# A planner's charge for TensorE's turns between kinds of matmul, in an attention and expert feed-forward kernel

## The reference, cut to what matters

```python
def _L0_xattn_ref(query, key, value, mask, Wq, Wk, Wv, Wo, Wg, bg):   # 2048 queries, 1601 keys, 16 heads of 16
    q, k, v = (heads of query @ Wq.T, key @ Wk.T, value @ Wv.T)
    scores = jnp.einsum('bhqd,bhkd->bhqk', q, k) / jnp.sqrt(jnp.float32(dk))
    scores = jnp.where(mask[:, None, None, :] == 0, neg_inf, scores)
    scores = jnp.where(future[None, None, :, :], neg_inf, scores)
    attn = jnp.nan_to_num(jax.nn.softmax(scores, axis=-1), nan=0.0)
    context = jnp.einsum('bhqk,bhkd->bhqd', attn, v)
    gate = jax.nn.sigmoid(query @ Wg.T + bg)
    return gate * context @ Wo.T
def _L0_ffn_ref(x, gate_w, w1, w2, w3):                                # 8 experts of 128, two per token
    scores = jax.nn.softmax(xf @ gate_w, axis=-1)
    scale = (the two largest scores of a token, 0 elsewhere)
    xs = scale.T[:, :, None] * xf[None, :, :]
    h = jax.nn.silu(einsum('etd,edh->eth', xs, w1)) * einsum('etd,edh->eth', xs, w3)
    return einsum('eth,ehd->etd', h, w2).sum(axis=0)
x = x + _L0_xattn_ref(_layernorm(x), ctx_1024, ctx_1024, mask_BxS2_ik0, ...)
x = x + _L0_ffn_ref(_layernorm(x), ...)
```

## Time and profile before

| | us |
| --- | --- |
| median of 3 runs | 680.01 |
| lowest and highest of them | 677.1, 682.3 |
| span of the profiled execution, first to last instruction | 676.9 |
| TensorE matmul busy | 644.6 (95%) |
| VectorE busy | 471.3 (70%) |
| ScalarE busy | 379.5 (56%) |
| POOL busy | 230.4 (34%) |

### The profile page before, as it was taken

The page is one execution under the profiler, slowest core; times in us unless marked ns, Lnnn a source line. Parts: engine busy times, 40 slices in busy tenths (PEclk is TensorE's granted clock), DMA queues, the critical chain, the costliest instruction groups (busy, mean ns, idle before and its releaser), DMA issues.

```text
span 676.9 us, 13559 instructions
## 1 busy us (share of the span) xinstructions
PE 644.6 (95%) x5320; PEld 393.0 (58%) x5320; DVE 471.3 (70%) x981; ACT 379.5 (56%) x778; POOL 230.4 (34%) x283
## 2 busy tenths in 40 slices
PE   7887999999999999999999999999999999979997
PEld 3363565555565545554565556455456766768885
DVE  6637779998989999999989987412205533676454
ACT  2221456766646676667646677877784565123332
POOL 5005212522123115021005033385434434536662
PEclk9878799999999999999999899999999999999999
DMA  6985982010260000010093010102101021104100
GB/s 170 234 133 115 138 144 31 2 22 24 69 68 1 3 1 3 1 65 2 14 161 109 2 34 3 35 2 78 32 32 32 17 63 49 31 16 109 48 32 31
DMA packets 29305, 36.58 MB, mean 54 GB/s; under 512 B 5833, under 2 KB 16457, under 8 KB 29242
## 3 DMA queue, kind: packets, MB, share of 16 engines
q1 hardware_dynamic: 26248, 34.53, 24.6%
q10 hardware_dynamic: 946, 0.92, 0.4%
q0 software_dynamic: 2048, 0.27, 0.3%
HBM read 25.58 MB, written 8.06 MB: 50 GB/s over the span
## 4 chain that ended last, share of the span: by engine, by line
PE 45%; DVE 12%; ACT 3%; POOL 2%; issue 1%; DVEq 0%; ACTq 0%; POOLq 0%
PE bank L1600 9%; DVE pmax L1303 9%; PE bank L1578 8%; PE bank L1664 4%; PE bank L1666 4%; PE bank L1665 4%; PE bank L1429 3%; PE bank L1545 3%; PE bank L1685 2%; PE bank L1686 2%; ACT probs L1160 2%; PE bank L1688 2%; DVE xn_sb L1274 1%; PE bank L1610 1%; PE bank L1583 1%
## 5 line engine op out<-in xcount | busy, mean ns | idle before, releaser
L1160 ACT ACTIVATE probs<-bank 128x512 f32<-128x512 f32 (+4 forms) x592 | 283.2, 555 | 147.0 <-PE bank L1578 87.5
L1303 DVE TENSOR_REDUCE pmax<-bank 128x1 f32<-128x512 f32 (+6 forms) x640 | 322.7, 574 | 29.4 <-PE bank L1549 15.9
L1578 PE MATMUL bank<-qaug,kaug 64*128 64x512 f32 (+4 forms) x592 | 151.6, 455 | 2.5 <-DVE pmax L1303 1.1
L1600 PE MATMUL bank<-probs,vaug 128*32 128x256 f32 (+4 forms) x2048 | 142.3, 390 | 2.2 <-ACT probs L1160 1.8
L1545 PE MATMUL bank<-kaug,qaug 62*128 62x512 f32 (+6 forms) x640 | 135.0, 404 | 9.8 <-DVE stage L807 3.4
L1578 PEld LDWEIGHTS bank<-qaug,kaug 64*128 64x128 f32 (+1 forms) x592 | 66.2, 183 | 85.7 <-ACT probs L1160 29.8
L1545 PEld LDWEIGHTS bank<-kaug,qaug 62*128 62x128 f32 x640 | 76.5, 189 | 40.7 <-DVE pmax L1303 21.0
L1600 PEld LDWEIGHTS bank<-probs,vaug 128*32 128x32 f32 (+1 forms) x2048 | 52.3, 109 | 53.3 <-ACT probs L1160 18.4
L1032 POOL TENSOR_TENSOR h_lo<-v_sb,h_hi 128x512 fp32r<-128x512 f32 x31 | 40.1, 1295 | 66.3 <-ACT h_hi L1216 66.3
L1396 DVE SCALAR_TENSOR_TENSOR v_sb<-t_sb,v_sb 128x512 f32<-128x512 f32 x32 | 24.2, 757 | 45.2 <-POOL v_sb L1028 38.2
L1216 ACT ACTIVATE h_hi<-v_sb 128x512 fp32r<-128x512 f32 x32 | 20.4, 637 | 57.4 <-DVE v_sb L1396 55.5
(11 more groups left out here) (143 smaller groups left out, 824.4 us busy)
## 6 DMA issues: line engine op xcount, KB each, us to landing
qaug<-s_dram SPq DMA_DIRECT2D x32, 256.0 KB, 3.4
qaug<-q_parts SPq DMA_DIRECT2D x18, 256.0 KB, 9.2
q_parts<-stage SPq DMA_DIRECT2D x7, 512.0 KB, 2.9
k_parts<-stage SPq DMA_DIRECT2D x4, 512.0 KB, 5.0
w_sb<-in_w SPq DMA_DIRECT2D x4, 512.0 KB, 10.0
out<-x_sb SPq DMA_DIRECT2D x8, 256.0 KB, 2.3
ctx_sb<-in_ctx_t SPq DMA_DIRECT2D x3, 512.0 KB, 6.4
x_sb<-in_x SPq DMA_DIRECT2D x3, 512.0 KB, 6.3
```

Of the source, the lines that this page charges most:

```text
L1160: act.activation(probs[0:rows, u % NSLOT, h, off:CH], bank_of(e)[0:rows, off:CH], ACT.Exp, scale=DK ** -0.5).then_inc(act_read, 1)
L1303: dve.tensor_reduce(pmax[:, n % 2, qt, h, slot:slot + 1], bank[:, 0:w], AX_X, ALU.max).then_inc(dve_read, 1)
L1578: last.append(pe.matmul(pair[side][0][0:r, off:CH], keys_at(b, ROWS, hp, P * j, r), qaug[b:b + ROWS, p % 2, hp, off:CH], start=True, stop= ...
L1600: last = pe.matmul(psum[O_BANK][32 * h:32 * h + 32, q0:q1], vaug[0:r, col:col + 32], probs[0:r, u % NSLOT, h, q0:q1], start=(j == 0), stop ...
```

## The change

Two constants of the planner. `SWITCH`, the delay of a step's start at a turn, goes from 100 ns to 0. `TURN`, the time that a turn adds to the step's end, goes from 150 to 140 ns into values and from 270 to 200 ns into scores; into other kinds it stays at 200.

```diff
-RELOAD, SWITCH, HOP, LOAD, PIECE = 107, 100, 2500, 9000, 3000
+RELOAD, SWITCH, HOP, LOAD, PIECE = 107, 0, 2500, 9000, 3000
 SPREAD = 0.6
-TURN = {"values": 150, "scores": 270, "other": 200}
+TURN = {"values": 140, "scores": 200, "other": 200}
```

## The result

The changed kernel takes 673.34 us in the median of 11 runs (669.82 to 682.9), the kernel before 680.33 in 11 runs (677.1 to 682.97). The ratio is 0.9913, 95% interval 0.989 to 0.9937: faster, by 0.9%, where 3% had been forecast. The profiled execution has a span of 670.2 us, for 676.9.

A forecast was written before the change was run, and what follows sets the result against it. No engine alone was taken to bound the middle: TensorE, VectorE and ScalarE wait for each other's turn at banks. Early 81, middle 390, late 183 and 3.6 us sum to 657.6 us of span, so a 660 us median, range 640 to 684.

The forecast's parts named there:

- The middle: From the second head group's last maximum to the last of all: 339.5 us TensorE work plus 50 waiting, 390 us.
- 47 of the 72 us: Middle's waiting before: 274 overcharged turns at about 0.17 us; near nothing after, the remaining 25 us doubled to 50.
- The early stretch: Up to the second head group's last maximum: set by loads and first projections, 81 us, at most 3 us either way.
- I take 9 us: 183 us: After the last maximum: 173.7 us of TensorE work plus 9 us waiting, where before 24 us were waited on 218.5.
- The 7 us on 86: Late stretch before, after the last scores, with experts and last chunk's routing: about 7 us waiting on 86.
- 42 us of passes beside 50 us: First eight experts: POOL's 42 us is under the 50 us of TensorE work between the first and last of them.
- The sum: Whole span: 81 + 390 + 183 + 3.6 = 657.6 us, for 676.9 before; the median about 660.
- A: Rival: VectorE alone sets the middle's pace, which stays 350 us; 621 us in all; chance 0.08.
- C: Rival, slower: waiting stays 21% of the middle, by rhythm of seven banks and in-order queues; 430 us, 701 total; chance 0.10.
- B: Rival: turns only replace waits, 20 us more work and 20 less waiting; 680 us (673 to 687); chance 0.12.

The follow-up runs named there:

- e17: The change with the last chunk's reads on ScalarE and the planner charged the score, values and turn prices the trace shows: 681.7 us, 1.001 against the kernel before.
- p_145_200: The change with 145 instead of 140 ns for a turn into values: 676.3 us, 0.994 against the kernel before.
- e1: The kernel before with only the start delay `SWITCH` taken from 100 to 0, `TURN` left as it was: 678.6 us, ratio 0.999.
- e16: The change with the product of two expert branches moved from POOL to VectorE for the first chunk's eight experts, planner told: 666.6 us, 0.978 against the kernel before.
- e15: The kernel before with the last chunk's four routing reads on ScalarE and its routing steps planned as ready later after the last maximum: 675.1 us, ratio 0.992.
- e12: The change with a start delay `SWITCH` of 50 ns instead of 0: 677.8 us, 0.995 against the kernel before.
- e10: The change with the last chunk's four bank reads of routing on ScalarE instead of VectorE: 667.9 us, 0.983 against the kernel before.
- e4: The kernel before with the new charges only for what is planned after the last maximum: 683.0 us, ratio 1.004.

## Why the prediction was right in sign and wrong in size

**The middle was right in its numbers.** Own work of 339.5 us was forecast and 342.6 is there, the stretch lasts 393.4 for 390, the last maximum comes at 469.5 (465 to 478), the first expert at 486.3 (485), VectorE's share is 82%. The turns cost what the earlier trace rows had shown.

**Its reason was not.** The step was that 47 of the 72 us waited are overcharged turns and that 25 doubled give 50. The 50 came out, but e17, planned with the measured prices, waits 54.6 (17.1 us of the stretch at the lower clock) and is no faster than the change at like clock, so the arithmetic through the charges is not what sets it. The 50 is luck. What e1, e17, p_145_200 and the change bear out is only that orders which alternate oftener wait 51 to 57 us instead of 68 to 71.

**The early stretch** was given as unchanged within 3 us. It is 68.2 us from TensorE's first step, for 73.7: 3.1 us more of own work and 8.6 less waiting. The term was 5.5 us too long. Half or more of that is the clock: the profiled execution of the change has 10.2 us at the lower clock there, the one before 20.5. Where it is 20.5 in both, e16 with the change's early order lasts 71.7 us and the old order 73.7 and 75.2 (before, e15). So some 2 to 3.5 us are the order's, about the 3 us that were allowed.

**The step that failed is "I take 9 us: 183 us" for the late stretch.** Its own work is 174.1 as forecast (173.7), the waiting 22.8. Two things were wrong in it. The 7 us on 86 of the part after the last scores were carried over from a part with no attention beside it, in which no weights are split any longer; the new order has the first chunk's experts, and their weights, there. And POOL was named as the danger but judged by its sum (42 us of passes beside 50 us of TensorE's work). The sum does fit; what the timelines show is two engines that work in order: a variance and a reciprocal root that end only behind a weight split, and a norm stretched beside two more passes, with TensorE waiting for the transpose. Taking eight products off POOL lowered late waiting by 7 us in the change (places of the routing steps included) and 2 in the kernel before. Place in the queue, VectorE's stretched steps and place in TensorE's order are not separated. Of the 22.8 us, up to 3.4 are the lower clock behind the two gaps (6.8 us of it), for which the sum had no term. The rest, 14 to 16 us, is spread over the end of attention, the routing steps and the last expert (2 us).

**The sum** misses by 12.6 us of span: 13.9 late, 3.4 in the middle, 5.5 the other way early, and the rest from where the cuts lie.

**The rivals.** A (the middle stays 350 us) and C (21% of waiting in the middle; it is 13%) are out. B, with 0.12, has the change's profile in most of its size (18.0 us more work for 24.7 less waiting), and e1's median; but at like clock e1 gains as the change does, so it is no case of B. That the clock would differ was in none of the rivals: e17, e1, e12, p_145_200 and the change have a mean of 0.965 to 0.975, the kernel before 0.978. It does not simply follow the number of turns, as e10 with 579 has 0.981 and e4 with 410 has 0.975. The Trainium skill says that a change of tiling mode drains TensorE ("TensorEngine Tiling (Array Packing)", Key Properties). The runs agree that turns cost, at 0.1 us each, and this takes most of what the better filling gives.

## What to carry to other kernels

When a planner is allowed to bring work forward, cost the stretch that it is taken from as carefully as the one that it goes to: what stood beside the first experts was cover, and 14 of the 20 us expected were lost there. Judge a loaded engine by what stands in its queue ahead of a short step on the critical chain, not by the sum of its work. When giving such steps more room only moves the waits, try taking work off the queue: here moving eight products of 1.3 us from POOL to VectorE, with the places that the planner then chose, took 7 us off the waiting. An experiment on a planned kernel changes the plan too, so compare the orders before giving the whole difference to the edit. Compare medians with the granted clock beside them: e1 and e17 seemed to gain nothing and had the change's gain at like clock.

## What the runs showed of the hardware

VectorE's operations on SBUF data alone were stretched while POOL ran its long passes. The variance step took 1.42 us beside POOL's weight split and ended with it (534.03 and 533.99), against 0.17 elsewhere. An expert's step on VectorE (L1396) took 2.68 us in e16 instead of 0.69, and ended 0.6 us after POOL's 2.82 us split (533.52 to 536.34). Four tiles of the norm, begun at 535.15, took 4.33 us and ended 0.8 us after the second of two POOL passes (L1028, then L1013 to 538.69); in e16, beside one, 2.06. On this the Trainium skill has a rule ("SBUF — State Buffer", Who interferes with whom): VectorE and GpSimd share one pair of ports; a VectorE step with two SBUF inputs contends with a GpSimd step that reads SBUF, a VectorE step in a two-port mode with GpSimd altogether, and whichever issues later waits for the whole of the earlier. The rows agree: L1396 at its usual 0.69 us behind 536.34 would end at 537.03, and ended at 536.90. No run isolates this mechanism.

The granted clock (first column after the five engines) in four stretches of the changed kernel:

```profile
208.00:214.90 6.90, 6.90 (x64) 4.89 (x58) 3.95 (x10) 3.41 (x8) 0.00 (x0) 1.00 0.00 1
215.00:221.60 6.60, 6.60 (x30) 2.80 (x29) 5.70 (x14) 2.50 (x7) 0.00 (x0) 0.50 0.01 2
539.30:542.50 3.20, 2.96 (x11) 2.76 (x12) 3.18 (x6) 1.24 (x2) 1.68 (x2) 0.50 0.01 4
556.40:559.60 3.20, 3.20 (x11) 2.50 (x9) 0.28 (x1) 1.22 (x2) 1.16 (x1) 0.50 0.03 5
```

It is at its lower level, 1.2 GHz, in the last three. At 539 and 556 us TensorE had stood idle for 4.65 and 2.55 us before or as it fell; with products at 0.43 instead of 0.23 us this added some 3 us to the two waits. In e16 the wait at the second norm is gone, and the products behind it are not slowed. A gap is not needed, though: at 215 us, and in e17 at 131 with 0.9 us idle before, the clock fell while TensorE was shown busy. What brought it down there no run shows.
